# Causal attention: maxima taken off in a spare row of the column products, and an unread 2-byte product in each slot

## The reference, cut to what matters

```python
h = _rmsnorm(x, ln1_w)
q = (h @ wq.T).reshape(Bx, Tx, NH, HD).transpose(0, 2, 1, 3)      # NH = 4 heads, HD = 16
k = (h @ wk.T).reshape(Bx, Tx, NKV, HD).transpose(0, 2, 1, 3)
q = q * cos + _rotate_half(q) * sin
k = k * cos + _rotate_half(k) * sin
scores = jnp.einsum('bhtd,bhsd->bhts', q, k) / jnp.sqrt(jnp.float32(HD))
scores = jnp.where(causal[None, None], scores, jnp.float32(-1e+30))
att = jax.nn.softmax(scores, axis=-1)
y = jnp.einsum('bhts,bhsd->bhtd', att, v).transpose(0, 2, 1, 3).reshape(Bx, Tx, Cx)
x = x + y @ wo.T
```

## Time and profile before

| what | value |
|---|---|
| median of 3 runs | 1157.09 us |
| the three runs | 1157.5, 1152.45, 1157.09 us |
| the profiled execution | 1154.18 us |
| its span | 1152.4 us |
| mean granted TensorE clock | 0.887 |
| TensorE busy | 972.5 us (84%) |
| VectorE busy | 685.9 us (60%) |
| ScalarE busy | 394.1 us (34%) |
| GpSimd busy | 166.4 us (14%) |

### The profile page before, as it was taken

One profiled execution on the slowest core, in us unless ns is written; L12 is line 12 of the kernel. 1 busy time (PEld: TensorE's weight loads), 2 busy tenths in 40 slices (PEclk: granted clock), 3 DMA queues, 4 the chain that ended last, 5 costly groups with the idle time before them and its releaser, 6 DMA issues. The chain is left out here.

```text
span 1152.4 us, 17992 instructions
## 1 busy us (share of the span) xinstructions
PE 972.5 (84%) x6791; PEld 503.0 (44%) x6791; DVE 685.9 (60%) x1757; ACT 394.1 (34%) x697; POOL 166.4 (14%) x179
## 2 busy tenths in 40 slices
PE   2898798879997856875968988999998789888998
PEld 1586577742233335652346442333333334443333
DVE  5966577865556247877464545555552545556665
ACT  1113422235552322322442442444444222343222
POOL 3500022214000023330040000111112102120000
PEclk9879777889999977997975997999998867889999
DMA  9200200000000001000000000000000000000000
GB/s 319 35 1 2 89 1 1 2 1 1 1 1 1 1 1 38 0 0 1 1 1 1 1 1 1 1 1 1 1 1 1 1 1 1 1 2 0 5 5 10
DMA packets 11473, 15.35 MB, mean 13 GB/s; under 512 B 8268, under 2 KB 9324, under 8 KB 10398
## 3 DMA queue, kind: packets, MB, share of 16 engines
q1 hardware_dynamic: 9976, 13.20, 3.7%
q10 hardware_dynamic: 1418, 1.09, 0.4%
HBM read 13.76 MB, written 0.52 MB: 12 GB/s over the span
## 5 line engine op out<-in xcount | busy, mean ns | idle before, releaser
L563 DVE TENSOR_REDUCE mx<-PS 128x2 f32<-128x1024 f32 (+3 forms) x104 | 109.6, 1096 | 102.5 <-PE PS L405 92.2
L525 ACT ACTIVATE arena<-PS 128x1024 f32<-128x1024 f32 (+3 forms) x104 | 91.1, 924 | 138.9 <-PE PS L435 138.9
L1061 DVE TENSOR_TENSOR arena<-arena,PS 128x512 f32<-128x512 f32 (+1 forms) x144 | 96.1, 686 | 66.5 <-ACT arena L1036 63.3
L1737 PE MATMUL PS<-identh 128*128 128x512 bf16 x343 | 97.0, 448 | 33.5 <-PEq L379 11.0
L979 PE MATMUL PS<-XT,late 64*128 64x512 f32 (+1 forms) x288 | 98.9, 636 | 6.8 <-PEq L1519 4.8
L447 PE MATMUL PS<-arena 128*64 128x512 f32 (+3 forms) x416 | 103.0, 586 | 0.5 <-ACT arena L516 0.4
L430 PE MATMUL PS<-arena 32*128 32x512 f32 (+4 forms) x416 | 82.6, 654 | 9.7 <-ACT arena L511 7.4
L634 POOL TENSOR_TENSOR H<-H,arena 128x256 f32<-128x256 f32 x36 | 26.2, 727 | 388.5 <-DVE arena L593 386.0
L1036 ACT ACTIVATE arena<-PS,f_b_sb 128x512 f32<-128x512 f32 x96 | 61.9, 686 | 58.4 <-PE PS L979 58.3
L405 PE MATMUL PS<-arena 32*128 32x512 f32 (+4 forms) x416 | 76.4, 662 | 5.9 <-POOL arena L623 2.9
L1003 PE MATMUL PS<-arena,late 128*64 128x512 f32 (+1 forms) x288 | 79.1, 617 | 0.4 <-DVE arena L1061 0.3
(11 more groups left out here) (402 smaller groups left out, 1665.8 us busy)
## 6 DMA issues: line engine op xcount, KB each, us to landing
arena<-in_rel SPq DMA_DIRECT2D x4, 1024.0 KB, 12.0
late<-in_edges SPq DMA_DIRECT2D x2, 1024.0 KB, 11.3
late<-in_w_f_w SPq DMA_DIRECT2D x3, 342.0 KB
arena<-in_adj SPq DMA_DIRECT2D x1, 1024.0 KB, 6.8
late<-in_w_f_w SPq DMA_DIRECT2D x2, 512.0 KB, 3.7
Cc<-in_consts SPq DMA_DIRECT2D x1, 914.0 KB
arena<-in_ids ACTq DMA_DIRECT2D x1, 800.0 KB
late<-in_w_f_w SPq DMA_DIRECT2D x4, 128.0 KB, 3.4
```

The lines of the kernel that those rows point to most:

```text
L525: nc.scalar.activation(PT[:, s % 2, p, :, queries(c)], PS[:, a:a + 2, queries(c)], ACT.Exp, scale=scale).then_inc(exp_done.sem, 1)
L563: v.reduce_max(mx[:, g % 2, c, 2 * p:2 * p + 2], PS[:, a:a + 2, keys(c)], axis=AX.X).then_inc(max_done.sem, 1)
L1061: nc.vector.tensor_tensor(HG[0:rows, n % 4, :], ha, PS[0:rows, gate_bank(n), :], ALU.mult).then_inc(gated_done.sem, 1)
L1737: nc.tensor.matmul(PS[:, 6, :], identh[:], bc(identh[:], 1, TB), start=True, stop=True, skip_group_check=True)
```

## The change

In the causal call only:

1. `unread(n, a)` issues n products of the 2-byte identity with itself, 512 columns, into a bank that is overwritten afterwards. One stands ahead of each pair's row products and one ahead of each pair's column products (64 in all), and five ahead of the wait for the values at the call's start.
2. The maxima go through a spare row of each head. VectorE's maximum is written as a 4-byte number into partition-wise zeros (`MF`, row 16 of each head's 32), TensorE transposes that tile, and VectorE subtracts it from the rotated queries (`lowered`); the keys have a 1 in that row. The column products then have the maxima taken off. The five splitting steps, ScalarE's copy and the second product of each head go away, and the exponential of a pair can start when that pair's column products are done.

```diff
+ "spare": 1 in CONSTS, ahead of "cos"
+        at["sin"][KD * h + HD] = 1.0
+    at["spare"][:, 0] = r % KD == HD
...
+    MF = part(8192, [2, TB, P])
...
+                def unread(n, a):
+                    for _ in range(n):
+                        nc.tensor.matmul(PS[:, a, :], identh[:], bc(identh[:], 1, TB), start=True, stop=True, skip_group_check=True)
+
...
                     for p in range(NPAIR):
                         a = slot(("A", s, p))
+                        if causal:
+                            unread(1, a)
                         for j in range(2):
...
                 def maxima(g):
                     a = slot(("T", g, 0))
-                    eng.wait_ge(split_done.sem, at(split_done, 5 * g + 4))
+                    if rope:
+                        eng.wait_ge(max_done.sem, at(max_done, (g * TB + TB) * NPAIR - 1))
+                    else:
+                        eng.wait_ge(split_done.sem, at(split_done, 5 * g + 4))
                     for c in range(TB):
+                        if rope:
+                            ins = nc.tensor.transpose(PS[:, a, c * P:(c + 1) * P], MF[:, g % 2, c, :], ident)
...
                     for p in range(NPAIR):
                         a = slot(("B", s, p))
+                        if causal:
+                            unread(1, a)
                         for j in range(2):
                             h = rr(2 * p + j)
-                            nc.tensor.matmul(PS[:, a + j, queries(c)], KT[...], QT[...], start=True, stop=False, ...)
-                    for p in range(NPAIR):
+                            ins = nc.tensor.matmul(PS[:, a + j, queries(c)], KT[...], QT[...], start=True, stop=bool(rope), ...)
+                        if rope:
+                            ins.then_inc(cols_done.sem, 1)
+                    for p in range(0 if rope else NPAIR):
...
                 ins.then_inc(vo_turned.sem, 1)
+                if causal:
+                    unread(5, 6)
                 eng.wait_ge(vo_ready.sem, at(vo_ready, 6))
...
-                v.memset(M3[:], 0.0).then_inc(vo_ready.sem, 1)
+                v.memset(MF[:] if rope else M3[:], 0.0).then_inc(vo_ready.sem, 1)
...
-                        v.tensor_tensor(RS[:, k, :], PS[:, a + 1, :], rope[1], ALU.mult).then_inc(roped.sem, 1)
+                        if k == 0:
+                            v.tensor_tensor(RS[:, k, :], PS[:, a + 1, :], rope[1], ALU.mult).then_inc(roped.sem, 1)
+                        else:
+                            v.scalar_tensor_tensor(out=RS[:, k, :], in0=PS[:, a + 1, :], scalar=rope[2], in1=rope[1], op0=ALU.add, op1=ALU.mult).then_inc(roped.sem, 1)
...
+                        if rope and g >= 2 and c == 0:
+                            eng.wait_ge(max_turned.sem, at(max_turned, g - 2))
+                        to = MF[:, g % 2, c].rearrange("p (h r) -> p h r", r=hr)[:, 2 * p:2 * p + 2, hr // 2] if rope else mx[:, g % 2, c, 2 * p:2 * p + 2]
+                        v.reduce_max(to, PS[:, a:a + 2, keys(c)], axis=AX.X).then_inc(max_done.sem, 1)
-                    if c == TB - 1:
+                    if c == TB - 1 and not rope:
...
+                def lowered(g):
+                    if rope:
+                        eng.wait_ge(max_turned.sem, at(max_turned, g))
+                        q = QT[:, g % 3, :]
+                        v.tensor_tensor(q, q, PS[:, bank(("T", g, 0)), :], ALU.subtract).then_inc(max_ready.sem, 1)
...
                 for s in range(TB):
                     maxima(s)
+                lowered(0)
...
                     if c == 1 and g >= 1:
                         outs(g - 1)
+                    if c == 3 and g + 1 < G:
+                        lowered(g + 1)
```

More of the change, by code:

```diff
@@ L60, in bc @@
     return ap.unsqueeze(axis).to_broadcast(shape)
-CONSTS = {"ident": 128, "twin": 64, "pick": 16, "drop": 64, "last": 1, "lower": 128, "causal": 128, "iota": 128, "col": 1, "heads": 64, "cos": 512, "sin": 512, "hi": 16, "bins": 32, "own": 32, "eps": 2}
+CONSTS = {"ident": 128, "twin": 64, "pick": 16, "drop": 64, "last": 1, "lower": 128, "causal": 128, "iota": 128, "col": 1, "heads": 64, "spare": 1, "cos": 512, "sin": 512, "hi": 16, "bins": 32, "own": 32, "eps": 2}
 def constants():
@@ L416, in maxima @@
                     a = slot(("T", g, 0))
-                    eng.wait_ge(split_done.sem, at(split_done, 5 * g + 4))
+                    if rope:
+                        eng.wait_ge(max_done.sem, at(max_done, (g * TB + TB) * NPAIR - 1))
+                    else:
+                        eng.wait_ge(split_done.sem, at(split_done, 5 * g + 4))
                     for c in range(TB):
-                        ins = nc.tensor.transpose(PSh[:, a, c * P:(c + 1) * P], M3[:, g % 2, c, :], identh[:])
+                        if rope:
+                            ins = nc.tensor.transpose(PS[:, a, c * P:(c + 1) * P], MF[:, g % 2, c, :], ident)
+                        else:
+                            ins = nc.tensor.transpose(PSh[:, a, c * P:(c + 1) * P], M3[:, g % 2, c, :], identh[:])
                     ins.then_inc(max_turned.sem, 1)
@@ L427, in cols @@
                         a = slot(("B", s, p))
+                        if causal:
+                            unread(1, a)
                         for j in range(2):
                             h = rr(2 * p + j)
-                            nc.tensor.matmul(PS[:, a + j, queries(c)], KT[h, g % 3, c * P:(c + 1) * P], QT[h, g % 3, queries(c)], start=True, stop=False, skip_group_check=True)
-                    for p in range(NPAIR):
+                            ins = nc.tensor.matmul(PS[:, a + j, queries(c)], KT[h, g % 3, c * P:(c + 1) * P], QT[h, g % 3, queries(c)], start=True, stop=bool(rope), skip_group_check=True)
+                        if rope:
+                            ins.then_inc(cols_done.sem, 1)
+                    for p in range(0 if rope else NPAIR):
                         a = bank(("B", s, p))
@@ L509, in maxima @@
                 def maxima(g):
+                    if rope:
+                        return
                     eng.wait_ge(max_turned.sem, at(max_turned, g))
@@ L562, in maxima @@
                         eng.wait_ge(rows_done.sem, at(rows_done, s * NPAIR + p))
-                        v.reduce_max(mx[:, g % 2, c, 2 * p:2 * p + 2], PS[:, a:a + 2, keys(c)], axis=AX.X).then_inc(max_done.sem, 1)
-                    if c == TB - 1:
+                        if rope and g >= 2 and c == 0:
[3 more added lines that the diff above has]
+                    if c == TB - 1 and not rope:
                         m, rest = mx[:, g % 2, :, 0:nh], mrest[:, g % 2, :, 0:nh]
@@ L646, in softmax_attention @@
         for signal, k in ((vo_turned, 1), (vo_ready, 7), (proj_done, G * PU), (roped, 2 * PU * G if rope else 0), (qk_ready, 2 * G), (rows_done, U * NPAIR),
-                          (max_done, U * NPAIR), (split_done, 5 * G), (max_turned, G), (max_ready, G), (cols_done, U * NPAIR), (exp_done, U * NPAIR), (later_zeroed, U * NPAIR if causal else 0),
+                          (max_done, U * NPAIR), (split_done, 0 if rope else 5 * G), (max_turned, G), (max_ready, G), (cols_done, U * NPAIR), (exp_done, U * NPAIR), (later_zeroed, U * NPAIR if causal else 0),
                           (mixed, G * NPAIR), (ctx_ready, G * NPAIR), (heads_out, G * NPAIR), (norm_step, G * NPAIR), (heads_normed, G * NPAIR),
@@ L2513, in l3_ffn @@
         softmax_attention(4, B, lambda g, j: g, project, MV[:, 0:4 * D], lambda g, p: p, R, X, 0.25,
-                          causal=(causalh[:], C["lower"]), rope=(C["cos"], C["sin"]))
+                          causal=(causalh[:], C["lower"]), rope=(C["cos"], C["sin"], C["spare"]))
         entry([Norm(X, R, eps=1e-6, center=False, gamma=row("f3_ln2"), plus=(Y, H, X))], turned=XT2[:],
```

## The result

The change makes the kernel slower: 1210.91 us (median of 4 runs, 1210.85 to 1214.62) against 1154.92 us for the kernel before in the same comparison, a ratio of 1.0492 with the 95% interval 1.0456 to 1.0529. The forecast of 1184 us had the sign right and half of the size; the measured time lies above its range.

What follows compares the result with a forecast made beforehand. TensorE was taken to bound the causal call. The lead-in's 6.9 and the groups' 11.0, 2.2, 5.5 and 4.0 sum to 29.6 us, added to the profiled 1154.2 for a forecast of 1184 us, range 1162 to 1200.

Steps and rivals of the forecast that it cites:

- What bounds the kernel: Causal call: TensorE, busy some 93% of each group, sets the pace; every added product is paid unless it fills a wait.
- The price of a slot: Row and column steps: unread product 0.32 us plus pair 1.05 us, 1.37 us at 512 columns and full clock.
- Group 1: Second of the causal call's four groups, all at full clock: 29.1 us for 26.91, +2.2.
- the lead-in: Projections and first row steps before the groups, with row steps at half clock: +6.9 us.
- the main term: Row and column steps: the full-height unread product makes the two pairs run in sequence; 0.36 of 0.68 us per slot.
- Group 0: First group: begins at half clock, which rises just after the second 512-column mixing; 36.5 us for 25.42, +11.0.
- Once up, I let it stay up: Waits between groups: 0.8 us without a product among long full-array work leaves the clock full; no time added.
- groups 2 and 3: Last two groups at full clock: 25.2 us for 19.66, +5.5, and 16.9 for 12.87, +4.0.
- The waits between groups, where it fell before: Kernel before: claimed the clock fell at the waits between groups, with two stretches, 40 us in all, at 1.2 GHz.
- the clock goes on falling between groups: Rival for the waits between groups: two 13 us stretches at half clock, +11, 1195 us; chance 0.15.
- Removed products counted as time alone: Column products lose their second product, those of the maxima; booked as time saved, with no effect on the clock.
- The faster rival: Slots cost only 0.21 us each, four heads side by side, full clock from group 0: -11.9, 1142 us; chance 0.09.

Runs made afterwards that it cites:

- e5_gap_filled: Changed kernel with three more unread products in each wait between groups, ahead of the wait for the lowered queries: 1187.88 us, ratio 1.0309.
- e3_unread_first: Changed kernel with both unread products of a step ahead of both pairs, same count and columns: 1149.81 us, ratio 0.9978.
- e7_head_rows: Changed kernel with each slot's unread product over 32 rows, those of its pair's first head: 1149.03 us, ratio 0.9974.
- e2_unread_alone: Kernel before plus only the unread products, one in each slot and five at the start, maxima as before: 1186.6 us, ratio 1.0283.
- e4_own_rows: Changed kernel with each slot's unread product over the 64 rows of its own pair: 1214.56 us, ratio 1.0528.
- e6_gap_only: Changed kernel without the 64 slot products, with three unread products in each wait between groups: 1146.84 us, ratio 0.9959.
- e1_no_slot_unread: Changed kernel without the 64 unread products of the slots; new maxima and five products at the start stay: 1152.07 us, ratio 0.9995.

## Why the prediction was right or wrong

**What bounds the kernel: right.** TensorE has a product under way for 97 to 98% of each group, and every product added to its stream was paid.

**The price of a slot: right at full clock.** 0.32 us for the unread product and 1.06 for a pair of 512 columns, forecast 0.32 and 1.05. At the lower level the pair took 2.01 us for the 1.86 taken from four side by side, 0.15 too little. Group 1 took 29.09 us for 29.1, the lead-in 31.19 for 31.2 (24.3 + 6.9). `e5_gap_filled` has group 2 at 25.19 for 25.2. That the second pair would lose its place beside the first, the main term, was right and is shown by `e3_unread_first` and `e7_head_rows`.

**Group 0: right in kind, too small.** I let the clock rise "just after the second" mixing of 512 columns, about 961; it rose at 970.6, just after the projection that follows (966.17 to 969.89). The term came out at +15.0 for +11.0. The reading behind it was that mixing had brought the clock back in the trace of before. It had done so among steps with four heads side by side; with two heads at a time the same mixing did not.

**"Once up, I let it stay up": wrong, and the step that failed.** I argued that the waits between groups hold 0.8 us without a product "among long full-array work". The wait was sized well (0.78 us), its surroundings were not: behind it stand not long full-height products but two slots whose pairs fill half of the rows. In `e3_unread_first`, with four heads side by side behind each of the same three waits of 0.78 us, the clock stayed full. In the changed kernel groups 2 and 3 came out 17.7 and 6.1 us beyond the forecast, with group 0's 4.0 some 28 us, which takes 1184 to about the measured time.

A misreading stood behind that step. "The waits between groups, where it fell before" is not what the trace of before shows: the stretch at 0.50 in the earlier trace rows begins at 955, and the wait between the groups ends only at 958.80. The clock was down some 3 us before that wait began, behind two shorter waits (0.48 and 0.64 us) and the column products of 128 columns. It did so again at 982.1, a third spell of 6.8 us that the 40 us of the forecast leave out. The line that shows the second of the two shorter waits:

```profile
953.96 0.38 PE L430 MATMUL PS<-arena 32*128 32x128 f32 x2 [0.64 <-DVE mx L563]
```

**The rival "the clock goes on falling between groups"** was the one that came, at a chance of 0.15 and a price of +11. Its price was wrong too. I took two spells of 13 us, as in the trace of before. In the changed kernel one spell of 54.6 us came: neither the slots nor single mixings of 512 columns (1021.42, 1028.10) ended it; it ended at 1066.2, after two such mixings in a row with no slot between them.

**Removed products counted as time alone.** The second column products cost 0.2 to 0.3 us a step, and I booked their removal as a gain. `e2_unread_alone` keeps them and its clock does not fall between groups 1 and 2. Two of them start beside the second pair (1012.96, where that pair starts at 1012.94), so that for a while four heads run at once; the other two follow at 1013.90. That they, and not the somewhat shorter wait there (0.68 against 0.78 us), hold the clock up was not tried by itself and stays open; that filling the waits suffices is shown.

**The faster rival (1142 us), 0.09:** its mechanism, four heads side by side and a full clock with the slot products, is nearly what `e3_unread_first` builds. That took 1149.8 us, not 1142. Its groups came to 80.8 us, where the rival had 73.0: it let a slot cost 0.21 us and no wait, and the trace has 0.54 us for the two unread products of a step and, in the groups, 4.5 us of waiting for free slots.

## What to carry to other kernels

A filler product is free only where the engine would wait anyway: here nine of them in three waits were worth some 20 us, and 64 of them in the stream cost 34. Before putting one between others, look at whether its neighbours run side by side and whether it has their tile height, and put it ahead of the whole set if not. And when a change removes or splits products, ask what it does to the clock at the next short wait, not only how long the removed ones took: a forecast that lets the clock stay where it is should carry the case in which it falls and does not come back.

## What the runs showed of the hardware that I had not expected

- Products of 64 rows and products of 32 rows on other rows of the array do not overlap at all (`e4_own_rows`: 1.37 us from pair to pair). Two 32-row 2-byte products and two 32-row 4-byte products start within 0.03 us of each other, and the whole step of six takes 1.18 us at 512 columns (`e7_head_rows`).
- A product of 32 columns and one of 512 both add the same 0.11 us of gap when they change the tile height at full clock (0.12 and 0.32 us to the next pair, less 0.013 and 0.213 of columns).
- TensorE can be busy for 53.22 of 54 us and stay at 1.2 GHz throughout, with a full-height 512-column product in every slot (the changed kernel, 1012 to 1066).
- A wait of 0.78 us can decide over 54.6 us of clock, or do nothing: at the end of group 0 the clock stayed up, at the end of group 1 it fell, with the same products around it. Why the two differ is open.
- Three unread products of 512 columns brought a fallen clock back within 0.4 to 0.8 us of the start of the first (`e6_gap_only`, 958.5 and 982.4), where without them it stayed down for 13.7 us (`e1_no_slot_unread`).
